# A product moved between two engines, three row passes moved by ten steps and one matmul pair issued a step earlier, in a fused selective-scan and mixture-of-experts kernel

## The chip, the cores and the metric

The kernel runs on one NeuronCore of a Trainium2 chip. The metric is the device time of one execution in microseconds (us); less is better. The engines are named as in the profile: PE (TensorE, matmuls), PEld (its weight loads), DVE (VectorE), ACT (ScalarE), POOL (GpSimd) and SP (SyncE, which issues DMAs).

## The reference

Eight sequences of 512 tokens with 256 channels. The first layer is a selective scan, the second a mixture of experts with top-1 routing and a shared expert. Cut to what matters:

```python
h = layernorm(x) * norm_w + norm_b
h = h @ in_proj_w.T                                   # 256 -> 512 channels
h = silu(causal_conv4(h, conv_w))
proj = h @ x_proj_w.T                                 # 1 + 16 + 16 columns
dt_in, B, C = proj[..., :1], proj[..., 1:17], proj[..., 17:]
dt = softplus(dt_in @ dt_proj_w.T + dt_proj_b)        # per channel
A = -exp(A_log)                                       # 512 channels x 16 states
state = exp(A * dt_t) * state + B_t * h_t             # scan over 512 tokens
y = (state * C_t).sum(states) + D * h_t
out = silu(y) @ out_proj_w.T + x
x1 = x + layernorm(out)
...
x2 = x1 + layernorm(shared(xn) + expert[argmax(xn @ gate_w)](xn * score))   # xn = layernorm(x1)
```

## The kernel before, in words

All data are fp32. The program has two stages. In the scan stage an outer loop i runs over the eight sequences (NB = 8), and in each iteration 32 steps q (Q = 32) run: two halves of the channels (2 x 128 channels each) times 16 states. The second stage, the experts, is not touched by the change.

One step q of the scan is spread over four engines. ACT makes the decays `exp(A*dt)` in PSUM (line 793, two activations, two decay buffers, made two steps ahead). The product B x h, called product q here, goes to a ring of four `bx` buffers. For the steps in `BY_POOL` (the even ones but one) POOL makes it four steps ahead, from rows of B that a DMA has broadcast (line 506). For the others DVE makes it right behind scan q - 1 (line 1114), from a row of B that PE has broadcast over the partitions into the one PSUM bank `psB` with a pair of matmuls (`spread_b`, line 1531); PE waits for DVE's product before it, since there is one bank. DVE scans (line 1126). POOL multiplies the state by C (line 517), and PE adds the states up with matmuls against an identity (`total`, line 1574), three steps behind.

Into the same 32 steps the work for the next sequence (`front`, i + 1) and for the previous one (`back`, i - 1) is written out by hand: `if q == ...` on each engine. So the order on each queue is fixed in the program, an engine does its instructions in that order, and a wait on one holds up all that stands behind it. On each engine in an iteration:

- PE: at q the loss or the spread for q + 2, then `back` at 15 and 17, then `total` for q - 3, then `front` at q. `front` 10 is the dt-in group, eight matmuls of `xp` (line 1447), `front` 18 the `w_bc` group, eight matmuls (line 1455). The `loss` for chunk c (q = 19, 21, 23, 25; lines 1522 and 1523) writes `lt - dt` into `psB` too, and the next spread waits until DVE's `min` has read it (`min_done`).
- ACT: the decays for q + 2, then at 9 the SiLUs of `front` and `back` with two table loads; at 11 and 12 two reads each of the dt-in group (`z`, line 687); at 13 to 17 softplus in five passes over 2048 elements (lines 696 to 708), the last one the `Ln` that gives `soft_ready`; at 19 first the copy of the `w_bc` group to `prow` (line 693, waits for `proj_ready`) and then the square of line 712 (`sq_ready`). For the sequence after the next (`lead`) it makes sums and squares of the rows of `xin` (line 641): sums at 3 to 6, a square at 7, three at 10.
- DVE: scan q, product q + 1 where it isn't POOL's, parts of `back` at 16, 18, 22, 24, 25, then `front`: convolution taps at 3, 5, 7 and 9 (line 1062) and the `min` of the loss at 19, 21, 23, 25 (line 1075), which waits for `loss_made` and `sq_ready`.

In i = 0 there is no `back`; in i = 7 there is no `front` and no loss, and PE does parts of the shared expert in its place (`early`, line 1552; DVE reads them at line 1104). `lead` exists in i = 0 to 5.

Of the kernel before, what the change touches and what calls it, by code (L numbers as in the profile page):

```python
# [19 lines left out]
def build(nc, x, winT, conv_w, xprojT, dt_w, dt_b, A_log, D, woutT, norm_w, norm_b,  # L20
# [16 lines left out]
    CH = C // H  # L37
    Q = H * N
    PN = N // 2
    BY_POOL = [q % 2 == 0 and q not in (14,) for q in range(Q)]  # L40
    PQ = sum(BY_POOL)
    DQ = Q - PQ
    NTH_P = [sum(BY_POOL[:q]) for q in range(Q + 1)]
    NTH_D = [q - sum(BY_POOL[:q]) for q in range(Q + 1)]
    RD = 2
# [3 lines left out]
    LOSS_AT = (19, 21, 23, 25)  # L49
# [19 lines left out]
    with ctx:  # L69
# [418 lines left out]
        def _(pool):  # L488
# [31 lines left out]
            def iteration(i, par, do_front):  # L520
                for q in range(Q):
                    if BY_POOL[(q + RB) % Q]:
                        if q + RB < Q:
# [84 lines left out]
        def _(act):  # L608
# [6 lines left out]
            def moments(i, b, mvt, scale=1.0, eps=epsc, sign=-1.0):  # L615
                nc.scalar.activation(lnv[i][:], mvt[:, :, 1], ACT.Ln, bias=eps[:], scale=scale)
                nc.scalar.activation(nmr[i][:], mvt[:, :, 0], ACT.Identity, scale=sign).then_inc(rs_ready[i], 1)
                act.wait_ge(rs_ready[i], 3 * b + 1)
                nc.scalar.activation(rstd[i][:], lnv[i][:], ACT.Exp, scale=-0.5).then_inc(rs_ready[i], 1)
                act.wait_ge(rs_ready[i], 3 * b + 2)  # L620
                for j in range(J):
                    last = nc.scalar.activation(nmr[i][:, j:j + 1], nmr[i][:, j:j + 1], ACT.Identity,
                                                scale=rstd[i][:, j:j + 1])
                last.then_inc(rs_ready[i], 1)
                act.wait_ge(rs_ready[i], 3 * b + 3)
# [3 lines left out]
            def apply(i, dst, src, js):  # L629
                for j in js:  # L630
                    last = nc.scalar.activation(dst[:, j % dst.shape[1], :], src[:, j, :], ACT.Identity,
                                                scale=rstd[i][:, j:j + 1], bias=nmr[i][:, j:j + 1])
                return last

            def lead(f, par, q):
                def row_pass(k, func, bias, dst):
                    if k == 0:
                        act.wait_ge(mv0_ready, f)
                    else:
                        act.wait_ge(row_passes, (2 * J - 1) * (f - 2) + k)  # L640
                    nc.scalar.activation(unused[:], xin[:, k % J, :], func, bias=bias,
                                         accum_out=dst).then_inc(mv0_ready if k == 2 * J - 1 else row_passes, 1)

                if q in (3, 4, 5, 6):
                    j = q - 3
                    if j == 0:
                        act.wait_ge(x_loaded, 16 * (f + 1))
                    row_pass(j, ACT.Identity, 0.0, xsum[:, j:j + 1])
                if q == 7:
                    act.wait_ge(row_passes, (2 * J - 1) * (f - 2) + J)  # L650
                    nc.scalar.activation(mv0[par][:, :, 0], xsum[:], ACT.Identity,
                                         scale=-1.0 / DIM).then_inc(mean_ready, 1)
                    act.wait_ge(mean_ready, f - 1)
                    row_pass(J, ACT.Square, mv0[par][:, 0, 0:1], mv0[par][:, 0, 1:2])
                if q == 10:
                    for j in range(1, J):
                        row_pass(J + j, ACT.Square, mv0[par][:, j, 0:1], mv0[par][:, j, 1:2])
                if q == 24:
                    act.wait_ge(mv0_ready, f + 1)
                    moments(3, f, mv0[par], (1.0 + EPS) / DIM, eps2c, 1.0)  # L660
                if q == 30:
                    if not (isinstance(f, int) and f == 0):
                        act.wait_ge(dt_ready, C * f)
                    apply(3, h1, xin, (0, 1))
                if q == 31:
                    apply(3, h1, xin, (2, 3)).then_inc(h1_ready, 1)
# [130 lines left out]
            def iteration(i, par, do_lead, do_front, do_scan, do_back):  # L797
                for q in range(Q):
# [29 lines left out]
                    if do_lead:  # L828
                        lead(i + 2, par, q)
# [190 lines left out]
        def _(dve):  # L1020
# [90 lines left out]
            def inject(i, par, q):  # L1111
                h, n = divmod(q, N)
                dve.wait_ge(b_bcast, i * DQ + NTH_D[q] + 1)
                nc.vector.tensor_tensor(bx[q % RB][:], xh[par][:, h * CH:(h + 1) * CH],  # L1114
                                        psB[:].unsqueeze(1).broadcast_to([P, CH, L]), ALU.mult).then_inc(dve_bx, 1)

            def scan(i, q):
                k = i * Q + q
                if BY_POOL[q]:
                    dve.wait_ge(pool_bx, i * PQ + NTH_P[q] + 1)  # L1120
                else:
                    dve.wait_ge(dve_bx, i * DQ + NTH_D[q] + 1)
                dve.wait_ge(decay_ready, k + 1)
                if not (isinstance(k, int) and k < RS):
                    dve.wait_ge(summed, k - RS + 1)
                nc.vector.tensor_tensor_scan(st[q % RS][:].rearrange("p c t -> p (c t)"),  # L1126
                                             decay[q % RD].rearrange("p c t -> p (c t)"),
                                             bx[q % RB][:].rearrange("p c t -> p (c t)"),
                                             0.0, ALU.mult, ALU.add).then_inc(scanned, 1)

            def iteration(i, par, do_lead, do_front, do_scan, do_back, do_choose=True):
                for q in range(Q):
                    if do_scan:
                        scan(i, q)
                        if q + 1 < Q and not BY_POOL[q + 1]:
                            inject(i, par, q + 1)
# [236 lines left out]
        def _(pe):  # L1373
# [144 lines left out]
            def loss(f, par, q):  # L1518
                c = LOSS_AT.index(q)
                pe.wait_ge(soft_ready, f + 1)  # L1520
                pe.wait_ge(dve_bx, (f - 1) * DQ + NTH_D[q + 1])
                nc.tensor.matmul(psB[:], ident[:], lt[:, c], start=True, stop=False)
                nc.tensor.matmul(psB[:], minus[:], dt[par][:, c], start=False, stop=True).then_inc(loss_made, 1)
# [54 lines left out]
            def total(i, par, q):  # L1578
                h, n = divmod(q, N)
                pe.wait_ge(weighted, i * Q + q + 1)  # L1580
                if n == 0 and not (isinstance(i, int) and i == 0 and h == 0):
                    pe.wait_ge(y_kept, H * i + h)
                if n == 0:
                    tiles(xh[par][:, h * CH:(h + 1) * CH], lambda half, c: dD[half, h * CH + c], True, False)
                tiles(st[q % RS], lambda half, c: ident[half, half], False, n == N - 1).then_inc(summed, 1)

            def iteration(i, par, do_front, do_scan, do_back):
                for q in range(Q):
                    if do_front and q - 1 in LOSS_AT:
                        pe.wait_ge(min_done, 2 + C * i + LOSS_AT.index(q - 1) + 1)  # L1590
                        spread_b(i, par, q + 1)
                    if do_front and q in LOSS_AT:
                        loss(i + 1, 1 - par, q)
                    elif not BY_POOL[(q + 2) % Q]:
                        if q + 2 < Q:
                            if do_scan:
                                spread_b(i, par, q + 2)
                        elif do_front:
                            spread_b(i + 1, 1 - par, q + 2 - Q)
                    if do_back and q in (15, 17):  # L1600
                        back(i - 1, q, do_front)
                    if do_scan and q >= SUM_LAG:
                        total(i, par, q - SUM_LAG)
                    elif do_back:
                        total(i - 1, 1 - par, q + Q - SUM_LAG)
                    if do_front:
                        front(i + 1, 1 - par, q)
                    else:
                        early(q)
                    if do_back and q not in (15, 17):  # L1610
                        back(i - 1, q, do_front)
                    if q == 20 and i >= 2:
                        choose(i - 2)

            first_front()
            iteration(0, 0, True, True, False)
            iteration(1, 1, True, True, True)
            for i in range(2, NB - 2):
                iteration(i, i % 2, True, True, True)
# [171 lines left out]
```

## Time and profile before

| | us |
|---|---|
| median of three runs | 1394.33 |
| lowest and highest | 1393.41 and 1395.83 |
| the profiled execution | 1393.79 |
| its span in the profile | 1392.0 |

The scan stage runs from about 50 to 972 us of the span, the experts follow. One iteration of the scan stage takes about 114 us. The mean granted clock of TensorE over the span is 0.968 of full speed. Views of the profile give idle time before an instruction and the instruction that ended it ("releaser"); where an instruction waits for several, the last one is named.

### The profile page before, as it was taken

To read this page: it belongs to the slowest core of one execution; us is meant where nothing else is said; L and a number is where in the kernel's file an instruction comes from. 1 tells how busy PE (TensorE), PEld (TensorE's weight loads), DVE (VectorE), ACT (ScalarE), POOL (GpSimd) and SP (SyncE) were. 2 spreads that over 40 slices of the span, in tenths; PEclk is the share of its full clock that TensorE was granted. 3 is DMA by queue.
4 is the path that set the end of the run, shared out by engine and by line. 5 is a ranking of instruction groups with operands and counts; after the bars stand their busy time and mean duration, and the time that the engine had idled before them with its cause. 6 is when DMAs were issued, how large, how long until landed. Compare 5 with 4: busy or idle time off the path is not lost.

```text
span 1392.0 us, 15477 instructions
## 1 busy us (share of the span) xinstructions
PE 1194.2 (86%) x4894; PEld 535.3 (38%) x4895; DVE 1069.5 (77%) x1409; ACT 796.5 (57%) x1386; POOL 1045.7 (75%) x558
## 2 busy tenths in 40 slices
PE   5668978887996996997798798898999999999995
PEld 2222223222332432432332243243545656656663
DVE  4588899999999999899999998799241116677675
ACT  5757679779778877877967875736431111111111
POOL 0579999999999999899999999989033723554453
PEclk9889999999999999999999999999999999999998
DMA  3921210330340141042034015001278522222220
GB/s 109 277 69 60 94 61 1 122 138 0 103 157 0 63 152 46 14 140 106 1 108 137 0 63 207 20 1 55 82 270 291 180 64 73 86 79 79 84 63 15
DMA packets 72068, 127.67 MB, mean 92 GB/s; under 512 B 8759, under 2 KB 48448, under 8 KB 67904
## 3 DMA queue, kind: packets, MB, share of 16 engines
q1 hardware_dynamic: 60432, 103.72, 22.2%
q0 software_dynamic: 7152, 16.81, 3.8%
q10 hardware_dynamic: 4416, 6.29, 1.3%
q8 instruction: 34, 0.56, 0.2%
q14 instruction: 34, 0.28, 0.1%
HBM read 97.79 MB, written 31.76 MB: 93 GB/s over the span
## 4 chain that ended last, share of the span: by engine, by line
PE 59%; DVE 21%; ACT 12%; issue 5%; DMA 1%; DVEq 0%; POOLq 0%; POOL 0%; ACTq 0%; SPq 0%
DVE state L1126 11%; PE psX L1697 10%; PE psY L1574 10%; PE psX L1632 5%; PE bank L1531 5%; DVE bx L1114 5%; PE bank L1487 4%; ACT psX L793 3%; PE psY L1645 3%; PE bank L1714 2%; PE psY L1714 2%; PE bank L1469 2%; PE bank L1470 2%; PE bank L1471 2%; DMA xin<-in_x 1%
## 5 line engine op out<-in xcount | busy, mean ns | idle before, releaser
L517 POOL TENSOR_TENSOR state<-state,cbc 128x1024 f32<-128x1024 f32 x256 | 599.2, 2367 | 10.2 <-DVE state L1126 10.2
L1126 DVE TENSOR_TENSOR_SCAN state<-psX,bx 128x1024 f32<-128x1024 f32 x256 | 580.9, 2282 | 25.9 <-ACT psX L793 22.2
L793 ACT ACTIVATE psX<-dt,aneg 128x511 f32<-128x511 f32 x512 | 331.3, 680 | 166.4 <-DVE state L1126 166.0
L506 POOL TENSOR_TENSOR bx<-xh,bbc 128x1024 f32<-128x1024 f32 x120 | 284.8, 2374 | 89.3 <-DVE state L1126 47.1
L1574 PE MATMUL psY<-state,ident 64*64 64x512 f32 x2048 | 268.0, 617 | 0.0
L1531 PE MATMUL bank<-prow,ident 128*128 128x512 f32 x272 | 151.0, 638 | 59.4 <-DVE bx L1114 57.5
L1114 DVE TENSOR_TENSOR bx<-xh,bank 128x1024 f32<-128x1024 f32 x136 | 162.9, 1198 | 15.4 <-PE bank L1531 15.3
L998 ACT ACTIVATE sg<-psX 128x512 f32<-128x512 f32 x39 | 23.3, 597 | 196.6 <-PE psX L1697 191.4
L1574 PEld LDWEIGHTS psY<-state,ident 64*64 64x64 f32 x2048 | 61.9, 133 | 166.3 <-issue 118.4
L1531 PEld LDWEIGHTS bank<-prow,ident 128*128 128x128 f32 x272 | 44.7, 192 | 149.5 <-DVE bx L1114 107.8
L581 POOL DMA_INDIRECT ysl<-shared_rows,idx x39 | 40.3, 1034 | 80.7 <-DVE idx L1292 75.7
L1201 DVE TENSOR_TENSOR actS<-sg,psX 128x512 f32<-128x512 f32 x28 | 19.0, 685 | 103.4 <-ACT sg L948 95.1
L1440 PE MATMUL bank<-lt,win 128*128 128x512 f32 x112 | 57.3, 636 | 26.3 <-DVE acc L1062 24.7
L1697 PE MATMUL psX<-wg,xsT 128*128 x156 | 77.2, 617 | 1.3 <-DVE xsT L1277 0.6
L1697 PE MATMUL psX<-wu,xsT 128*128 x156 | 73.3, 592 | 0.0
L590 POOL DMA_INDIRECT result<-yo,idx x39 | 40.1, 1029 | 36.9 <-DVE yo L1340 29.3
L1062 DVE SCALAR_TENSOR_TENSOR acc<-bank,cw,acc 128x511 f32<-128x511 f32 (+2 forms) x84 | 62.2, 741 | 6.1 <-ACT acc L676 4.1
L1447 PE MATMUL bank<-xh,xp 128*128 128x512 f32 x56 | 40.2, 883 | 27.1 <-ACT xh L682 27.1
L1283 DVE TENSOR_TENSOR actN<-sg,psX 128x512 f32<-128x512 f32 x39 | 26.8, 687 | 44.1 <-ACT sg L998 40.3
L948 ACT ACTIVATE sg<-psX 128x512 f32<-128x512 f32 x28 | 16.5, 596 | 76.8 <-PE psX L1632 76.8
L561 POOL COPY xrow<-ids 128x4 f32<-128x4 f32 x8 | 1.6, 201 | 77.8 <-issue 55.4
L1487 PE MATMUL bank<-wout,yv 128*128 128x256 f32 x256 | 58.0, 380 | 2.3 <-ACT yv L739 2.2
(212 smaller groups left out, 1798.2 us busy)
## 6 DMA issues: line engine op xcount, KB each, us to landing
cbc<-bc_rows SPq DMA_DIRECT2D x32, 1024.0 KB, 6.6
bbc<-bc_rows SPq DMA_DIRECT2D x16, 1024.0 KB, 6.4
slot_in<-ao SPq DMA_DIRECT2D x1, 5011.5 KB, 35.2
xsl<-slot_in SPq DMA_DIRECT2D x39, 128.5 KB
xin<-in_x SPq DMA_DIRECT2D x8, 512.0 KB, 4.1
xr<-in_x SPq DMA_DIRECT2D x8, 512.0 KB, 5.5
x_rows<-ao SPq DMA_DIRECT2D x8, 512.0 KB, 3.4
xn_rows<-xr SPq DMA_DIRECT2D x8, 512.0 KB, 3.2
```

Source lines behind the costliest of these rows:

```text
L506: nc.gpsimd.tensor_tensor(bx[q % RB][:], xh[par][:, h * CH:(h + 1) * CH], bbc[:, n // 2].unsqueeze(1).broadcast_to([P, CH, L]), ALU.mult). ...
L517: nc.gpsimd.tensor_tensor(w[:], w[:], cbc[:, n].unsqueeze(1).broadcast_to([P, CH, L]), ALU.mult).then_inc(weighted, 1)
L793: e = nc.scalar.activation(decay[q % RD][:, c, 1:L], dt[par][:, h * CH + c, 1:L], ACT.Exp, scale=aneg[:, h * CH + c, n:n + 1])
L1062: last = nc.vector.scalar_tensor_tensor(out=acc[:, c, m:L], in0=psF[:, 0:L - m], scalar=cw[:, c, TAPS - 1 - m:TAPS - m], in1=acc[:, c, m:L ...
L1114: nc.vector.tensor_tensor(bx[q % RB][:], xh[par][:, h * CH:(h + 1) * CH], psB[:].unsqueeze(1).broadcast_to([P, CH, L]), ALU.mult).then_inc ...
L1126: nc.vector.tensor_tensor_scan(st[q % RS][:].rearrange("p c t -> p (c t)"), decay[q % RD].rearrange("p c t -> p (c t)"), bx[q % RB][:].rea ...
L1440: last = nc.tensor.matmul(psF[:], win[:, k, c * P:(c + 1) * P], hT[:, k], start=(k == 0), stop=(k == KC - 1))
L1487: last = nc.tensor.matmul(psF[:, (j % 2) * DIM:(j % 2 + 1) * DIM], yv[:, c, j * P:(j + 1) * P], wout[:, c], start=(c == 0), stop=(c == C - 1))
L1531: nc.tensor.matmul(psB[:], ident[:, n:n + 1].broadcast_to([P, P]), prow[par][:], start=True, stop=True).then_inc(b_bcast, 1)
L1574: done = nc.tensor.matmul(psY[o * HP:(o + 1) * HP, r], weights(half, c), src[half, c], start=first, stop=last_)
L1632: last = nc.tensor.matmul(bank, w[:, k, c * P:(c + 1) * P], xg[g % 2][:, k], start=(k == 0), stop=(k == KC - 1))
L1697: last = nc.tensor.matmul(bank, xsT[i][:, k], w[:, bass.ds(ereg[i], 1), k].rearrange("p a n -> p (a n)"), start=(k == 0), stop=(k == KC - 1))
```

## The change

Three edits in the scan stage:

1. The one even step whose product DVE makes is 12 instead of 14. So POOL makes product 14, and PE spreads B for step 12 (issued at step 10) and no longer for step 14 (issued at step 12).
2. The three squares of `lead` on ACT stand at step 20 instead of step 10.
3. On PE the loss of chunk 0 (q = 19) is issued at step 18, behind `total` and ahead of `front` 18, instead of at the beginning of step 19. It keeps its waits: `soft_ready`, and DVE's products up to 19.

```diff
-    BY_POOL = [q % 2 == 0 and q not in (14,) for q in range(Q)]
+    BY_POOL = [q % 2 == 0 and q not in (12,) for q in range(Q)]
...
-                if q == 10:
+                if q == 20:
                     for j in range(1, J):
                         row_pass(J + j, ACT.Square, mv0[par][:, j, 0:1], mv0[par][:, j, 1:2])
...
                     if do_front and q in LOSS_AT:
-                        loss(i + 1, 1 - par, q)
+                        if q > LOSS_AT[0]:
+                            loss(i + 1, 1 - par, q)
                     elif not BY_POOL[(q + 2) % Q]:
...
                     elif do_back:
                         total(i - 1, 1 - par, q + Q - SUM_LAG)
+                    if do_front and q == LOSS_AT[0] - 1:
+                        loss(i + 1, 1 - par, q + 1)
                     if do_front:
                         front(i + 1, 1 - par, q)
```

## Rows read from the trace of the kernel before

**Rows 1.** The page, busy time of each engine over the span.

```profile
PE 1194.2 (86%) x4894; PEld 535.3 (38%) x4895; DVE 1069.5 (77%) x1409; ACT 796.5 (57%) x1386; POOL 1045.7 (75%) x558
```

**Rows 2.** Who waited for whom: us in total, times, longest.

```profile
DVE lt L1075 <- ACT yv L712: 20.4, 7, 3.0
```

**Rows 3.** Timeline of DVE, i = 3: start, duration, instruction, [idle before <-releaser].

```profile
439.73 1.20 DVE L1114 TENSOR_TENSOR bx<-xh,bank 128x1024 f32<-128x1024 f32 x1
...
444.47 2.29 DVE L1126 TENSOR_TENSOR_SCAN state<-psX,bx 128x1024 f32<-128x1024 f32 x1 [1.21 <-ACT psX L793]
446.68 1.20 DVE L1114 TENSOR_TENSOR bx<-xh,bank 128x1024 f32<-128x1024 f32 x1
...
473.99 0.69 DVE L1075 SCALAR_TENSOR_TENSOR lt<-bank,yv 128x512 f32<-128x512 f32 x1 [2.90 <-ACT yv L712]
```

**Rows 4.** Timeline of PE, i = 3, around the dt-in group.

```profile
434.20 1.95 PE L1574 MATMUL psY<-state,ident 64*64 64x512 f32 x16
440.02 5.31 PE L1447 MATMUL bank<-xh,xp 128*128 128x512 f32 x8 [3.88 <-ACT xh L682]
445.17 1.02 PE L1531 MATMUL bank<-prow,ident 128*128 128x512 f32 x2
```

**Rows 5.** Windows: stretch, length, busy times, granted clock, DMA share, GB/s.

```profile
440.00:441.40 1.40, 1.38 (x2) 0.84 (x3) 1.37 (x2) 1.40 (x1) 1.40 (x2) 0.50 0.00 0
```

**Rows 6.** Timeline of PE, the dt-in group in i = 0, 2 and 5.

```profile
100.20 6.25 PE L1447 MATMUL bank<-xh,xp 128*128 128x512 f32 x8 [3.87 <-ACT xh L682]
...
324.97 6.51 PE L1447 MATMUL bank<-xh,xp 128*128 128x512 f32 x8 [3.88 <-ACT xh L682]
...
669.02 5.16 PE L1447 MATMUL bank<-xh,xp 128*128 128x512 f32 x8 [3.88 <-ACT xh L682]
```

**Rows 7.** Timeline of PE, i = 3, from the `w_bc` group on.

```profile
467.57 3.70 PE L1455 MATMUL bank<-xh,w_bc 128*128 128x512 f32 x8
471.11 1.02 PE L1522 MATMUL bank<-lt,ident 128*128 128x512 f32 x2
...
472.92 1.09 PE L1574 MATMUL psY<-xh,dD 64*64 64x512 f32 x8
```

**Rows 8.** Timeline of DVE, product 13 in i = 2 and scan 12 in i = 5.

```profile
332.38 1.22 DVE L1114 TENSOR_TENSOR bx<-xh,bank 128x1024 f32<-128x1024 f32 x1 [0.67 <-PE bank L1531]
...
673.82 2.29 DVE L1126 TENSOR_TENSOR_SCAN state<-psX,bx 128x1024 f32<-128x1024 f32 x1 [1.57 <-ACT psX L793]
```

**Rows 9.** Timeline of ACT, i = 3, steps 17 to 21.

```profile
464.58 1.91 ACT L708 ACTIVATE dt<-lt 128x2048 f32<-128x2048 f32 x1
...
471.12 1.30 ACT L793 ACTIVATE psX<-dt,aneg 128x511 f32<-128x511 f32 x2 [2.33 <-DVE state L1126]
472.36 0.58 ACT L693 ACTIVATE prow<-bank 128x512 f32<-128x512 f32 x1
472.84 1.05 ACT L712 ACTIVATE yv<-tmp 128x1024 f32<-128x1024 f32 x1
...
480.41 1.30 ACT L793 ACTIVATE psX<-dt,aneg 128x511 f32<-128x511 f32 x2 [0.76 <-DVE state L1126]
```

**Rows 10.** Timeline of DVE, i = 0: product 13 and the first `min`.

```profile
107.36 1.22 DVE L1114 TENSOR_TENSOR bx<-xh,bank 128x1024 f32<-128x1024 f32 x1 [1.73 <-PE bank L1531]
...
132.03 0.69 DVE L1075 SCALAR_TENSOR_TENSOR lt<-bank,yv 128x512 f32<-128x512 f32 x1 [3.02 <-ACT yv L712]
```

**Rows 11.** Timeline of DVE, i = 7: scan 12 and the second read of `early`.

```profile
903.55 2.29 DVE L1126 TENSOR_TENSOR_SCAN state<-psX,bx 128x1024 f32<-128x1024 f32 x1 [3.44 <-ACT psX L793]
...
912.77 0.69 DVE L1104 TENSOR_TENSOR acc<-bank,acc 128x512 f32<-128x512 f32 x1 [1.90 <-PE bank L1552]
```

**Rows 12.** Timeline of ACT, i = 3: the first of three squares, then decays 13.

```profile
444.32 0.49 ACT L641 ACTIVATE unused<-xin,mv 128x256 bf16<-128x256 f32 x1
...
446.08 1.28 ACT L793 ACTIVATE psX<-dt,aneg 128x511 f32<-128x511 f32 x2
```

**Rows 13.** Timeline of ACT, i = 0: the `Ln`.

```profile
125.19 1.90 ACT L708 ACTIVATE dt<-lt 128x2048 f32<-128x2048 f32 x1
```

## The prediction

> **What bounds the kernel now.** I read the page's busy shares first [rows 1], then the list of waits [rows 2], then the timelines of DVE, PE and ACT over one steady iteration of the outer loop (i = 3, from 398 to 512 us), and last the same places in i = 0 and i = 7. PE has the largest busy time over the whole span, but the change lies in the scan stage, and there the timelines show DVE nearly without a gap: every scan and every product follows the one before within 0.1 us, save at a few places. PE, ACT and POOL have gaps in each iteration. What DVE waits for in that stage is therefore what the time is made of. In i = 3 its large gaps are 1.21 us before scan 12 and 2.90 us before the first `min` [rows 3]. No gap of DVE's names POOL.
>
> First place. Scan 12 waits for its decays, which ACT makes late because the two SiLUs and two table loads of step 9 stand ahead of them. Product 13 follows without a wait [rows 3]. On PE the eight `xp` matmuls of `front`, step 10 (the dt-in group), run from 440.02, and the spread for product 13 only after them, at 445.17 [rows 4]; that is 1.5 us before DVE wants it. In that window TensorE's granted clock is 0.50 of full speed, the 1.2 GHz level, after 3.88 us in which PE did nothing [rows 4, 5]. The group takes 5.16 to 6.51 us over the seven iterations that have it [rows 4, 6] and about 3.7 us would be its time at 2.4 GHz, as the equally large `w_bc` group shows [rows 7]. Where it took 6.51 us, product 13 also waited 0.67 us [rows 8]. The mean gap of DVE at this place over i = 1 to 6 is 1.45 us: 1.2 in three, 1.6 in two (one of them is shown), 1.21 + 0.67 in one [rows 3, 8].
>
> Second place. DVE waits for `sq_ready`, not for the loss: ACT ends decays 21, copies `prow` and then squares, up to 473.9 [rows 9, 3]. The loss of chunk 0 has ended by 472.9, when PE's next group begins [rows 7]. The wait occurs in all seven iterations with a front, 20.4 us in all [rows 2].
>
> **The change, part by part.**
>
> *Product 12 to DVE, product 14 to POOL.* DVE's work per iteration is the same, 17 products of 1.20 us; so is POOL's. What moves is a spread on PE. Spread 12 is now issued at step 10, ahead of `total` and of the dt-in group, and it waits for product 11, which ends at 440.93 [rows 3]. All that stands behind it on PE waits too: `total` 7 (about 1.0 us, half of the 1.95 us for two [rows 4]) and the dt-in group, which could otherwise start at 440.02. Spread 13 needs product 12 and stands behind the dt-in group. I work this out for i = 3. PE starts at 441.0. At full clock: spread 12 takes 1.05, `total` 7 1.0, dt-in to the next group 3.55, spread 13 to the start of the product 1.05. Sum 6.65, so 447.65. To this comes half of the time that PE runs at half clock. From the duration of the group (half clock time = 2 x (duration - 3.70)) it was 2.9 us at least (5.16), 5.6 at most (6.51), and 4.1 in the mean of the seven. So product 13 can start at 447.65 + 2.05 = 449.7 (449.1 to 450.45).
>
> On DVE scan 11 ends at 443.2, product 12 then fills the gap until decays 12 are there (444.4), scan 12 ends at 446.7 as before, and product 13 now waits until 449.7: 3.0 us (2.4 to 3.8). Against the 1.45 us of before this is +1.55 us per iteration (+1.0 to +2.35): 9.5 us over i = 1 to 6. I take the mean since the row of each end is one of seven. In i = 0 there was no gap at scan 12 and 1.73 us at product 13 [rows 10]. By the same sum product 13 starts 9.2 us after 101.2 with the 5.1 us of half clock that its 6.25 us group shows [rows 6], at 110.4; scan 12 would end at 106.9; a wait of 3.5, thus +1.8.
>
> A rule of the Trainium skill bears on this ("TensorE: Matmul & The Clock Gate", Part 1, The HAM clock gate): the array's default is the throttled state at 1.2 GHz, only activity releases it, and how many matmuls run slow differs between runs with the phase in which they begin. The trace agrees: 0.50 granted, and 5.16 to 6.51 us for one and the same group. With PE at full clock the wait would be 1.0 us and this edit would gain 0.45 us per iteration.
>
> In i = 7 the dt-in group is absent. The gap before scan 12 is 3.44 us there, and product 12 fits in: 1.2 us less later on. PE then no longer has to do spread 14 between the second and third `shu` group, for which DVE waited 1.90 us [rows 11]. That gives up to -3.1; bounds 0 and -3.1. I take -3.0, since both gaps are in the rows and spread 12, which waits for product 11 only, has all of scan 11 to run in.
>
> POOL makes product 14 as soon as scan 10 is over, about 439.8 to 442.2, well ahead of scan 14. Scan 14 no longer has a product before it on DVE; decays 14 are due about 451.6, when the dt-in group (ends about 448.8) has been read twice by ACT, ahead of scan 14 at 453. Cost 0; if this cover went, scan 14 would wait what decays 14 are late.
>
> *The squares from step 10 to step 20.* Three row passes take 1.76 us of ACT (444.32 to 446.08) [rows 12]. At step 10 they delay nothing DVE waits for: decays 13 end at 447.36, and product 13 is over at 447.88. At step 20 ACT has 0.76 us idle before decays 23 [rows 9], so decays 23, the second square and the apply of step 21 come 1.0 us later. They are hidden by scan 22, product 23 and DVE's wait-free run behind them; I take 0. If this cover failed, 1.0 us in each of the five iterations with lead and back, +5. A gain is excluded, as step 10 is followed by a wait for the dt-in group in any case. No DMA moves: the next load of `xin` waits for `h1_ready` of step 31.
>
> *The loss of chunk 0 ahead of `front` 18.* Nothing is gained by an earlier loss, as `sq_ready` ends the wait. What the four matmuls delay is the `w_bc` group: it ran 467.57 to 471.2, the loss 471.11 to 472.92, 1.81 us [rows 7]. With the order turned the `w_bc` group ends at 473.05, and the `prow` copy, which began at 472.36 behind decays 21, begins at 473.1: +0.74 us for the copy, the square and the `min`. These stand in one queue on ACT. So +0.74 us per iteration, 4.4 us over six; bounds 0 (if some of it were made up) and 1.81 (no slack at all). The loss now also waits for `soft_ready`, the end of ACT's `Ln` [rows 9], and if that is late, `w_bc` is late behind it. In i = 3 the `Ln` ends at 466.4 and PE comes to the loss at 467.6. The delays of the first edit move PE by 1.6 and ACT by about the same (1.6 to 2.1), so 0.7 us of cover remain or more. In i = 0 PE comes there earlier, and `Ln` ends at 127.1 [rows 13]. Late by some 2.3 us more (my estimate, between DVE's 1.8 and the 3.0 of the dt-in group), it lets the loss start at 129.4; with 1.85 + 3.65 + 0.48 + 1.05 for loss, `w_bc`, copy and square the `min` starts at 136.5 against 132.0 [rows 10]: 4.4 in all, 2.6 of it by this edit beyond the 1.8 above.
>
> The sum: 9.5 + 1.8 - 3.0 + 0 + 4.4 + 2.6 = 15.3 us. Later gaps of DVE, at scan 30 and product 31, come from PE groups that start with DVE's products and so move along; nothing is given back there. What follows the scan stage moves as a whole. On the profiled execution's own 1393.8 us this makes 1409 us. The median of the three runs shown is 0.5 us above that execution.
>
> **The rivals.**
>
> *Faster: product 12 fills an empty place and product 13 isn't late.* For it speaks that the 1.21 us gap is real, and that spread 13 was over (446.2) 0.5 us before its use. Against it, PE's order: spread 13 is behind 3.7 us of matmuls that begin after 443. It decides if spread 13 is done by 446.7, that is if the dt-in group ends by 445.7. Then 6 x 1.45 + 1.7 + 3.0 = 13.4 are gained, 7.0 lost by the loss: 1387 us.
>
> *The clock stays at 2.4 GHz.* PE would be idle 5.7 us before 441, longer than the 3.88 us after which it was at half; so little speaks for it. Then the first edit gives 6 x -0.45, about -0.8 and -3.0, together -6.5 against +7.0: 1394 us.
>
> *The early loss costs nothing,* because ACT finds other slack: 1409 - 7 = 1402 us. Against it, copy and square are back to back [rows 9].
>
> *The dt chain on ACT becomes the bound.* If `Ln` ends more than 0.7 us later against PE than worked out, each iteration has loss, `w_bc`, copy and square behind it. With 1.2 us more in six iterations, or with the squares of step 20 not covered: 1415 to 1419 us.
>
> **How the numbers follow.** Forecast case 0.70 (1402 to 1417), the faster rival 0.07, full clock 0.05, loss free 0.08, dt chain 0.10. Less than 0.2% (2.8 us) can't be told from no change in a measurement of this kernel. Slower: 0.70 + 0.08 + 0.10 = 0.88; the same 0.05; faster 0.07. The bounds of the terms, taken together, give +7 to +26; as they would hardly all fall on one side, the range is 1399 to 1417.
>
> **What would show it.** In the profile after, DVE should have no gap before scan 12 and one of 2.4 to 3.8 us before product 13, released by PE's spread, in i = 1 to 6. PE should be idle about 5.7 us before spread 12, with the clock at 0.5 behind it. The gap before the first `min` should be 3.6 us instead of 2.9, still released by the square of ACT, and more than 5 us in i = 0. In i = 7 the gap before scan 12 should be 2.2 us. The prediction is wrong if product 13 follows scan 12 at once, or if the `prow` copy begins with the end of decays 21.

## The result, and the profile after

The changed kernel takes 1422.94 us (median of four executions, 1417.17 to 1428.37) against 1394.76 us of the kernel before: ratio 1.0202, 95% interval 1.0146 to 1.0258. It is slower, as forecast, but by 28 us where 15 were forecast, and above the range of 1399 to 1417. The four executions lie in two groups, 1417.2 and 1417.7, 1428.2 and 1428.4. The profiled one is of the first: 1417.67 us, span 1415.9, which is 23.9 more than the span before.

What the prediction asked for is there in i = 3. Timeline of DVE in the changed kernel; the columns are start, duration, instruction and, in brackets, the idle time before it and what ended it:

```profile
403.91 2.29 DVE L1126 TENSOR_TENSOR_SCAN state<-psX,bx 128x1024 f32<-128x1024 f32 x1 [0.77 <-ACT psX L793]
...
458.85 1.22 DVE L1114 TENSOR_TENSOR bx<-xh,bank 128x1024 f32<-128x1024 f32 x1 [2.39 <-PE bank L1531]
...
485.63 0.69 DVE L1075 SCALAR_TENSOR_TENSOR lt<-bank,yv 128x512 f32<-128x512 f32 x1 [3.60 <-ACT yv L712]
...
520.29 2.29 DVE L1126 TENSOR_TENSOR_SCAN state<-psX,bx 128x1024 f32<-128x1024 f32 x1 [0.77 <-ACT psX L793]
...
576.72 1.22 DVE L1114 TENSOR_TENSOR bx<-xh,bank 128x1024 f32<-128x1024 f32 x1 [3.88 <-PE bank L1531]
...
589.94 0.69 DVE L1084 TENSOR_TENSOR ao<-bank,ao 128x512 f32<-128x512 f32 x1 [0.77 <-PE bank L1487]
...
605.13 0.69 DVE L1075 SCALAR_TENSOR_TENSOR lt<-bank,yv 128x512 f32<-128x512 f32 x1 [4.08 <-ACT yv L712]
```

The gap before scan 12 [rows 3] is gone. Product 13 waits 2.39 us for PE's spread, and the first `min` waits 3.60 us for the square instead of 2.90 [rows 3]. The first and the fourth line are scan 30 of i = 2 and of i = 3: an iteration of 116.38 us. The last three lines belong to i = 4. Product 13 waits 3.88 there, DVE's `add` behind product 17 waits 0.77 for the out-projection, which it did not before, and the `min` waits 4.08. That iteration takes 119.50 us, 3.1 more than i = 3. Of these, 1.5 are the longer wait of product 13; the waits of two `add`s (0.77 and 0.20, none in i = 3) and the longer one of the `min` are another 1.45.

PE shows what differs. Its timeline, i = 3 and then i = 4:

```profile
450.69 2.07 PE L1531 MATMUL bank<-prow,ident 128*128 128x512 f32 x2 [5.70 <-DVE bx L1114]
...
454.25 3.70 PE L1447 MATMUL bank<-xh,xp 128*128 128x512 f32 x8
...
465.75 1.12 PE L1531 MATMUL bank<-prow,ident 128*128 128x512 f32 x2 [2.12 <-DVE bx L1114]
...
567.07 2.07 PE L1531 MATMUL bank<-prow,ident 128*128 128x512 f32 x2 [5.70 <-DVE bx L1114]
...
570.98 4.84 PE L1447 MATMUL bank<-xh,xp 128*128 128x512 f32 x8
...
583.61 2.08 PE L1531 MATMUL bank<-prow,ident 128*128 128x512 f32 x2 [2.12 <-DVE bx L1114]
...
585.48 4.35 PE L1487 MATMUL bank<-wout,yv 128*128 128x256 f32 x16
```

In both, PE is idle 5.70 us ahead of spread 12, as worked out. The dt-in group then runs for 3.70 us in the one and 4.84 us in the other. And in both PE is idle 2.12 us ahead of spread 17. In i = 3 that spread takes 1.12 us, in i = 4 2.08. The windows of the changed kernel there (stretch, length, PE busy, granted clock, DMA share, GB/s):

```profile
465.70:467.00 1.30, 1.25 (x4) 1.00 0.00 0
...
583.60:584.60 1.00, 0.99 (x1) 0.50 0.00 0
```

The clock has fallen to 1.2 GHz a second time, in i = 4 to 6 but not in i = 1 to 3. The same instructions in the same order make an iteration of either kind. In what follows, a long iteration is one with this second fall.

The lengths of the iterations, from scan 30 to scan 30, and what each adds to the span (i = 0 is the shift of scan 30 in it, i = 7 the rest up to the end):

| | i=0 | 1 | 2 | 3 | 4 | 5 | 6 | i=7 | sum |
|---|---|---|---|---|---|---|---|---|---|
| before, us | | 113.68 | 114.96 | 114.27 | 114.74 | 114.62 | 114.27 | | |
| after, us | | 117.01 | 116.60 | 116.38 | 119.50 | 119.47 | 119.23 | | |
| difference | +4.7 | +3.3 | +1.6 | +2.1 | +4.8 | +4.9 | +5.0 | -2.5 | +23.9 |
| forecast | +4.4 | +2.3 | +2.3 | +2.3 | +2.3 | +2.3 | +2.3 | -3.0 | +15.3 |

For i = 0 and i = 7 the timeline of DVE after the change has:

```profile
136.76 0.69 DVE L1075 SCALAR_TENSOR_TENSOR lt<-bank,yv 128x512 f32<-128x512 f32 x1 [5.67 <-ACT yv L712]
...
930.52 2.29 DVE L1126 TENSOR_TENSOR_SCAN state<-psX,bx 128x1024 f32<-128x1024 f32 x1 [2.33 <-issue]
```

against 3.02 us [rows 10] and 3.44 us [rows 11]. The wait of 1.90 us for the second `shu` group [rows 11] is gone.

### The profile page after: what moved, and what is told of

It reads as the page before. It is cut to its first block, busy times and chain, and to the rows that moved or that the text cites. A ratio compares the mean times of both kernels' runs of the same rounds, so it can differ in the third digit from the quotient of the medians.

```text
span 1415.9 us, 15477 instructions
## 1 busy us (share of the span) xinstructions
PE 1198.8 (85%) x4894; PEld 535.7 (38%) x4895; DVE 1069.9 (76%) x1409; ACT 797.0 (56%) x1386; POOL 1045.6 (74%) x558
## 4 chain that ended last, share of the span: by engine, by line
PE 58%; DVE 23%; ACT 11%; issue 5%; DMA 2%; DVEq 0%; POOLq 0%; POOL 0%; ACTq 0%; SPq 0%
DVE state L1126 13%; PE psX L1700 10%; PE psY L1574 8%; PE bank L1531 5%; PE psX L1635 5%; DVE bx L1114 4%; PE bank L1487 4%; ACT psX L793 3%; PE psY L1648 3%; PE psY L1717 2%; PE bank L1717 2%; DVE acc L1062 2%; PE bank L1469 2%; PE bank L1447 2%; PE bank L1455 2%
## 5 line engine op out<-in xcount | busy, mean ns | idle before, releaser
L1574 PE MATMUL psY<-state,ident 64*64 64x512 f32 x2048 | 272.6, 627 | 0.0
L1531 PE MATMUL bank<-prow,ident 128*128 128x512 f32 x272 | 161.2, 677 | 102.2 <-DVE bx L1114 94.8
L1487 PEld LDWEIGHTS bank<-wout,yv 128*128 128x128 f32 x256 | 50.5, 198 | 18.6 <-issue 9.2
```

Of the source, the lines that this page charges most:

```text
L1487: last = nc.tensor.matmul(psF[:, (j % 2) * DIM:(j % 2 + 1) * DIM], yv[:, c, j * P:(j + 1) * P], wout[:, c], start=(c == 0), stop=(c == C - 1))
L1531: nc.tensor.matmul(psB[:], ident[:, n:n + 1].broadcast_to([P, P]), prow[par][:], start=True, stop=True).then_inc(b_bcast, 1)
L1574: done = nc.tensor.matmul(psY[o * HP:(o + 1) * HP, r], weights(half, c), src[half, c], start=first, stop=last_)
```

## The experiments

### One edit at a time

Each of these three kernels is the kernel before with one of the three parts of the diff.

> Only product 12 goes to DVE and product 14 to POOL. Theory: this edit alone carries the larger part of the loss, through two steps: product 13 waits 2.4 to 3.9 us behind the dt-in group, and in some iterations PE, idle 2.1 us before spread 17, falls to 1.2 GHz once more and comes late with the out-projection. +9 to +18 us against the kernel before, with a spread between executions. Rival: the second fall of the clock needs the early loss as well; then +8 us and no more, in every execution.

Measured: 1404.28 us, ratio 1.0067 (1.0054 to 1.0080), +9.2 us. Timeline of DVE, product 13 and the first `min` in i = 3:

```profile
457.23 1.22 DVE L1114 TENSOR_TENSOR bx<-xh,bank 128x1024 f32<-128x1024 f32 x1 [3.08 <-PE bank L1531]
...
483.31 0.69 DVE L1075 SCALAR_TENSOR_TENSOR lt<-bank,yv 128x512 f32<-128x512 f32 x1 [2.90 <-ACT yv L712]
```

Product 13 waits about 3 us, which was the mean forecast. The forecast for this edit was +8.3. No iteration is long: they take 115.47, 116.26, 116.20, 116.13, 116.08 and 116.06 us, although PE is idle 2.12 us ahead of each spread 17. The executions lie within 1403.6 to 1406.0. So this edit alone doesn't bring the second fall in the profiled execution, and the rival stated for this run holds, 1 us above its "no more".

> Only the three squares move from step 10 to 20. Theory: hidden at both places, within 2 us of the kernel before. Rival: the apply of step 21 comes late for DVE's add of step 22 and costs up to 1 us in each of five iterations, +3 to +5 us.

Measured: 1396.48 us, ratio 1.0011 (1.0003 to 1.0020), +1.4 us. The forecast was 0. In i = 1 DVE's `add` of step 22 waits for the apply that now stands behind the squares:

```profile
256.90 0.69 DVE L1094 TENSOR_TENSOR ao<-bank,xr 128x512 f32<-128x512 f32 x1 [0.56 <-ACT bank L631]
```

From the first `min` to scan 30 it takes 34.67 us there against 34.01 before, and 34.66 against 34.48 in i = 3: 0.66 + 4 x 0.18 = 1.4 us.

> Only the loss of chunk 0 goes ahead of the w_bc group. Theory: the prow copy on ACT begins 0.7 us later, and so the square and the min: gap of DVE before the first min 3.6 us instead of 2.9 in i = 1 to 6, some 5 us in i = 0; +6 to +7 us in all. Rival: ACT makes the delay up, and the run is within 2 us of the kernel before.

Measured: 1402.49 us, ratio 1.0055 (1.0042 to 1.0068), +7.4 us. The forecast for this edit was +7.0. The gap before the first `min` is that forecast, in each of i = 1 to 6; in i = 0 it was 8.18 us in the profiled execution, more than expected (5.2 us more than before, where 2.6 were stated for this edit). That execution is the longest of the five (1405.6), so the agreement of 7.4 with 7.0 is partly luck:

```profile
138.46 0.69 DVE L1075 SCALAR_TENSOR_TENSOR lt<-bank,yv 128x512 f32<-128x512 f32 x1 [8.18 <-ACT yv L712]
...
482.29 0.69 DVE L1075 SCALAR_TENSOR_TENSOR lt<-bank,yv 128x512 f32<-128x512 f32 x1 [3.60 <-ACT yv L712]
```

One by one the edits cost 9.2 + 1.4 + 7.4 = 18 us. Together they cost 22 to 34. What is missing is in the combination.

### Is it the clock?

```diff
+                    if do_front and q == 10:
+                        pe.wait_ge(conv_done, C * (i + 2))
+                        for _ in range(4):
+                            nc.tensor.matmul(psF[:], ident[:], win[:, 0, 0:512], start=True, stop=True)
```

> The changed kernel, and ahead of spread 12 PE does four idle matmuls of 512 columns into the free bank, whose results are overwritten, so that its clock doesn't fall there. Theory: the clock is the larger part of the product-13 wait (expected 1.0 us instead of 2.4 to 3.9) and of the second fall; 1396 to 1402 us. Rival: the order of PE's work by itself makes product 13 late, whatever the clock; 1409 us or more.

Measured: 1403.42 us, ratio 1.0063 (1.0050 to 1.0076). That is 14 to 25 us less than the changed kernel, by adding work. In i = 1 and 3 the clock holds, and product 13 waits what was worked out for the full clock, 1.0 us:

```profile
455.67 1.22 DVE L1114 TENSOR_TENSOR bx<-xh,bank 128x1024 f32<-128x1024 f32 x1 [1.02 <-PE bank L1531]
```

In i = 0, 2, 4 and 5 the gap before the idle matmuls is enough for the clock to fall; product 12 waits 0.6 to 0.7 us there, product 13 1.96. No iteration is long. The theory is right on the mechanism and a little too hopeful on the time (1396 to 1402).

> The changed kernel unchanged, for more executions and another profile. The profile so far has iterations of two lengths: about 116.5 us (i = 1 to 3) and 119.5 us (i = 4 to 6), the long ones with a second fall of the clock ahead of spread 17. Theory: executions differ in how many iterations are long: times between 1409 us (none) and 1429 us (all six), most at either end. Rival: the long executions lose their time somewhere else, for instance in the expert stage; then a profile of one shows the same iterations as before.

Measured: 1419.04 us, ratio 1.0182 (1.0155 to 1.0210). Four executions lie between 1417.9 and 1419.4, one at 1428.3, and none at 1409. The new profile is of one at 1419.4 and has the same three long iterations, i = 4 to 6 (119.63, 119.51 and 119.24 us). So in the shorter executions the pattern repeats and isn't drawn anew each time, against the first half of the theory. But three of the nine executions of this kernel take 1428 us, and none of them was profiled. The mean granted clock of each is on record: 0.958 in all three, 0.962 to 0.964 in the six shorter ones. So they spent more of their time at half clock.

```diff
+                    if do_front and q == 15:
+                        pe.wait_ge(z_done, i + 2)
+                        for _ in range(2):
+                            nc.tensor.matmul(psF[:], ident[:], win[:, 0, 0:512], start=True, stop=True)
```

> The changed kernel, and ahead of spread 17 PE does two idle matmuls of 512 columns into the free bank, so that the 2.1 us in which it waited for product 15 are filled. Theory: no second fall, all iterations about 116.5 us, 1409 to 1413 us with under 5 us between executions. Rival: the 3 us of the long iterations come from the late dt chain on ACT and not from PE's clock; then 1417 to 1428 us stay.

Measured: 1412.95 us (1411.1 to 1414.3), ratio 1.0128 (1.0112 to 1.0143). Timeline of PE in i = 4; L1592 are the two inserted matmuls, with spread 17 and the out-projection behind them:

```profile
571.36 4.86 PE L1447 MATMUL bank<-xh,xp 128*128 128x512 f32 x8
...
581.82 1.98 PE L1592 MATMUL bank<-win,ident 128*128 128x512 f32 x4
584.01 1.12 PE L1531 MATMUL bank<-prow,ident 128*128 128x512 f32 x2 [0.21 <-DVE bx L1114]
584.97 3.62 PE L1487 MATMUL bank<-wout,yv 128*128 128x256 f32 x16
```

The dt-in group is as slow as in the long iteration of the changed kernel (4.86 us, and product 13 waits 3.90 us), but spread 17 and the out-projection run at full clock. The iteration takes 117.90 us, no other takes more than 117.3. This shows what the second fall does: without it i = 4 takes 117.90 us and not 119.5, and i = 5 and 6 take 116.98 and 116.32 and not 119.5 and 119.2. The 1.5 us by which product 13 waits longer in i = 4 stay, as they stand ahead of the filled gap, but they no longer return in full in the next iterations (2.98 and 2.21 us of wait, against 3.86 and 3.50). It is 6 us against the median of the changed kernel's repetition (1419.04), and there is no second group among the four executions.

The same idea on the kernel before, with three matmuls at step 10:

> The kernel before with three idle matmuls on PE ahead of the dt-in group, so that this group runs at 2.4 GHz. Theory: the dt-in group is no bound there but in i = 0, 2 and 4 (waits of 1.7, 0.7 and 0.4 us), so 1391 to 1394 us. Rival: the idle matmuls delay total 6 or the dt-in group itself, and the time is the same or 1 to 3 us longer.

Measured: 1398.3 us, ratio 1.0018 (1.0009 to 1.0027). No gain; the rival was right: 3 us longer in the median. The profiled execution is the shortest (1395.7). Its timeline of PE in i = 2:

```profile
322.19 4.54 PE L1592 MATMUL bank<-win,ident 128*128 128x512 f32 x6 [2.39 <-DVE acc L1062]
...
327.67 3.70 PE L1447 MATMUL bank<-xh,xp 128*128 128x512 f32 x8
```

The dt-in group does run at full clock, 3.70 us where it took 6.51 [rows 6]. But the idle matmuls themselves take 4.54 us ahead of it, and product 13 waits 1.00 us behind it, 0.67 before [rows 8]. Over i = 1 to 6 product 13 waits 3.6 us in all, against 1.0 in the kernel before; only in i = 0 it waits less (0.63 against 1.73).

### Which of the edits brings the long iterations

The next kernel has parts 1 and 3 of the diff and leaves the squares at step 10.

> Product 12 to DVE and the early loss, without the move of the squares. The edits one by one gave +9.2, +1.4 and +7.4 us, together 18, and the changed kernel has +23 to +34. Theory: the second fall depends only on where in its rhythm the clock gate meets the gap ahead of spread 17, and this changes with every edit that changes the length of an iteration; so this kernel lies at 1411 to 1414 us, or has long iterations too. Rival: the squares at step 20 are needed for the long iterations because they delay ACT; then 1412 us in every execution.

Measured: 1408.1 us (1407.0 to 1409.1), ratio 1.0092 (1.0077 to 1.0108), below both numbers expected, and 3.8 us less than the 9.2 + 7.4 us of the two edits alone would give. No long iteration. The lengths are 116.85, 116.89, 116.51, 116.33, 116.19, 116.12 us: they fall from one to the next, and with them the wait of product 13, from 3.64 us in i = 1 to 2.45 in i = 5. So the move of the squares, which by itself costs 1.4 us, costs 9 to 20 us on top of the other two.

The next two add two or four statistics instructions in i = 0 to this kernel, the third adds two to the changed kernel:

```diff
+                        if isinstance(i, int) and i == 0 and q == 15:
+                            for k in range(2):
+                                nc.vector.bn_stats(out=bst[1][:, k, :], in_=xh[0][:, k, :])
```

> Product 12 on DVE and the early loss, without the move of the squares, and two statistics instructions of DVE on data that nobody reads, behind scan 15 of i = 0 only, about 1.4 us. They shift all later iterations against the rhythm of the clock gate and cost 1.4 us once. Theory: whether an iteration is long depends on this phase alone, so long iterations (119.5 us, a second fall ahead of spread 17) can appear without any change of the squares: a time above 1408 + 1.4 + 3 us, or, where this shift leads away from it, 1409 to 1410 us. Rival: the squares at step 20 are needed for them; then 1409.5 us and no long iteration in this run and in the one with four instructions.

> As the run before with four such instructions, about 2.8 us once. Theory: at least one of the two shifts brings long iterations, and then 1414 us or more. Rival: 1411 us and no long iteration.

> The changed kernel with the two statistics instructions in i = 0, 1.4 us later. Theory: with another phase the number of long iterations is another one than three (none: about 1411 us; all six: about 1429 us). Rival: the long iterations are i = 4 to 6 again, because something in these iterations itself makes them long; then 1419 us.

Measured: 1409.67 us, 1409.2 us and 1419.1 us (ratios 1.0107, 1.0104 and 1.0172). There is no long iteration in the first two, and the lengths again settle (116.11 and 116.08 us in i = 6). In the third the long ones are i = 4 to 6 again. So a shift of 1.4 or 2.8 us at the start does not decide it; my theory is wrong for these executions.

Two theories were left: the squares lengthen the iteration by 0.2 us, so that it doesn't settle at about 116.1 us; or it matters that they stand on ACT there. The next two kernels lengthen the iterations with the squares at step 10, by statistics over 64 and over 256 elements in every iteration with a front:

```diff
+                        if do_front and q == 22:
+                            nc.vector.bn_stats(out=bst[1][:, 0, :], in_=xh[par][:, 0, 0:64])
```

> Product 12 on DVE and the early loss, squares at step 10, and in each iteration with a front one statistics instruction of DVE over 64 elements on data that nobody reads, behind scan 22 (some 0.2 us, as much as the squares cost). Theory: it is the length of an iteration that brings the long ones, so they appear: 1415 us or more. Rival: only squares on ACT at step 20 bring them; then 1408 + 7 x 0.2 = 1410 us.

Measured: 1414.13 us (1414.1 to 1416.1), ratio 1.0143 (1.0127 to 1.0158). Timeline of DVE, the added instruction in i = 4, and product 13, the `add` and the `min` of i = 5:

```profile
610.75 0.20 DVE L1136 BATCH_NORM_STATS2 bst<-xh 128x6 f32<-128x64 f32 x1
610.87 1.20 DVE L1114 TENSOR_TENSOR bx<-xh,bank 128x1024 f32<-128x1024 f32 x1
...
692.38 1.22 DVE L1114 TENSOR_TENSOR bx<-xh,bank 128x1024 f32<-128x1024 f32 x1 [3.96 <-PE bank L1533]
705.64 0.69 DVE L1084 TENSOR_TENSOR ao<-bank,ao 128x512 f32<-128x512 f32 x1 [0.81 <-PE bank L1489]
...
720.83 0.69 DVE L1075 SCALAR_TENSOR_TENSOR lt<-bank,yv 128x512 f32<-128x512 f32 x1 [4.08 <-ACT yv L712]
```

An instruction that moves the next one by 0.12 us makes i = 5 and 6 long: the lengths are 116.84, 116.88, 116.56, 116.30, 119.52, 119.47 us. PE has the mark of the changed kernel:

```profile
699.27 2.08 PE L1533 MATMUL bank<-prow,ident 128*128 128x512 f32 x2 [2.12 <-DVE bx L1114]
```

Seven times 0.12 us have cost 6 us (the ratio to the kernel before is 1.0143, and 1.0092 without the instruction). (Line numbers of this kernel are up to two higher, by the added lines.)

> The same over 256 elements (about 0.35 us). Theory: long iterations from an earlier iteration on, 1418 us or more. Rival: 1411 us.

Measured: 1415.02 us, ratio 1.0147 (1.0131 to 1.0162). The long iteration comes earlier, in i = 4 (119.61 us), as the theory says. But then i = 5 takes 117.89 us and i = 6 116.97, so it isn't worse in all; the 1418 us or more did not come. How i = 4 and i = 5 differ is shown further down.

> The changed kernel with the three squares at step 23 instead of 20, behind the apply that DVE's add waits for, where ACT has room. Theory: they no longer lengthen the iteration, no long iterations, 1408 us as without their move. Rival: late squares bring long iterations wherever they stand; 1417 us or more.

Measured: 1408.22 us (1407.7 to 1411.1), ratio 1.0095 (1.0079 to 1.0110). The squares are later still and there is no long iteration (117.01, 116.97, 116.56, 116.35, 116.20, 116.13 us). Together with the run with statistics over 64 elements, this shows that the added length brings the long ones, and not the place of the squares on ACT. One digit in the changed kernel (`q == 23` for `q == 20`) takes 11 us off its median of 1419.

> Product 12 on DVE and squares at step 20, without the early loss. Theory: the length of the iterations of the first edit alone settles at 116.06 us; with 0.2 us more it may no longer, and long iterations appear: 1409 us or more. Rival: they need the early loss too; 1404.3 + 1.4 = 1405.7 us.

Measured: 1405.6 us, ratio 1.0079 (1.0065 to 1.0092), which is the sum of the two edits, and no long iteration; the rival holds. Without the early loss, 0.2 us more is still taken up: the lengths stay between 115.9 and 116.2 us, and product 13 waits less (2.42 to 3.03 us, against 2.60 to 3.22 with the first edit alone).

The traces of these runs show how the lengths come about. Behind the idle time ahead of spread 12 the clock is at half until it rises, and the longer that takes from the start of spread 12 on, the longer product 13 waits. Where narrow windows go from 0.50 to 1.00 is the time of the rise. For i = 3 and i = 4 of the changed kernel (stretch, length, PE busy, granted clock, DMA share, GB/s):

```profile
453.50:453.80 0.30, 0.30 (x8) 0.50 0.00 0
453.90:454.20 0.30, 0.30 (x4) 1.00 0.00 0
...
573.00:573.30 0.30, 0.30 (x2) 0.50 0.00 0
573.40:573.70 0.30, 0.30 (x2) 1.00 0.00 0
```

| changed kernel | i=1 | 2 | 3 | 4 | 5 | 6 |
|---|---|---|---|---|---|---|
| rise of the clock, us | 221.73 | 337.78 | 453.84 | 573.30 | 692.77 | 812.24 |
| spread 12 starts ahead of it by | 4.78 | 3.78 | 3.15 | 6.24 | 6.20 | 6.20 |
| product 13 waits | 3.16 | 2.70 | 2.39 | 3.88 | 3.86 | 3.50 |

(In i = 6 scan 12 itself waits too, 0.45 us, so product 13's wait is shorter.) In i = 1 to 3 the rises are 116.05 us apart while the iterations take 117.0 to 116.4 us. So spread 12 comes closer to the rise each time, and the wait shrinks. Then a rise comes 119.5 us after the last one, spread 12 again has a long stretch at half clock, and from there rises and iterations both go by 119.5 us. In the kernels that settle (product 12 and the early loss with or without instructions in i = 0, and the squares at step 23) the rises stay 116.05 us apart in i = 1 to 6, and the iterations come down to 116.1 us. With spread 12 about 3.1 us ahead of the rise, the kernel with the squares at step 10 takes 116.12 us, and the changed kernel still 116.38. That an iteration settles where it gets down to the distance of the rises, and otherwise slips until a rise comes later, is my reading of these rows; why a rise comes when it does no run shows.

The second fall goes by the same rise. There are twelve spreads 17 at half clock in the traces (three each in the two profiles of the changed kernel and in the one with two instructions in i = 0, two and one in the kernels with statistics over 64 and 256 elements). All twelve start 10.22 to 10.33 us after the rise. The 72 others with the same 2.12 us of idle time ahead of them start 10.37 us after it or later. The kernel with 256 elements has one of each, in i = 4 and i = 5, 10.29 and 10.37 us after the rise:

```profile
584.44 2.07 PE L1533 MATMUL bank<-prow,ident 128*128 128x512 f32 x2 [2.12 <-DVE bx L1114]
...
703.98 1.12 PE L1533 MATMUL bank<-prow,ident 128*128 128x512 f32 x2 [2.12 <-DVE bx L1114]
```

### A version that should have beaten both

```diff
-                if q == 19:
+                if q == 18:      # ACT: the square of line 712
...
-                    if do_choose and q == 21:      # DVE, and ahead of back
+                    if do_choose and q == 22:
...
-                    if q == 20 and i >= 2:         # PE
+                    if q == 21 and i >= 2:
```

> The kernel before with the square of step 19 on ACT moved to step 18, where ACT is idle 2.3 us, and the router's matmuls and their copy one step later (21 and 22), so that PE comes to the second loss sooner. Theory: the first min waits for the loss instead of the square, 0.9 us less, and the second min no longer for PE; 0.6 to 1.3 us less in each of six iterations, 1387 to 1392 us. Rival: PE is busy without a gap from spread 17 to the second loss, so the gain comes back as a wait for spread 23 or the second min: within 2 us of the kernel before.

Measured: 1401.43 us, ratio 1.0046 (1.0034 to 1.0058), +6.5 us. Timeline of DVE, i = 3:

```profile
472.07 0.69 DVE L1075 SCALAR_TENSOR_TENSOR lt<-bank,yv 128x512 f32<-128x512 f32 x1 [1.93 <-PE bank L1523]
...
482.23 1.22 DVE L1114 TENSOR_TENSOR bx<-xh,bank 128x1024 f32<-128x1024 f32 x1 [0.90 <-PE bank L1531]
...
484.74 0.69 DVE L1094 TENSOR_TENSOR ao<-bank,xr 128x512 f32<-128x512 f32 x1 [1.20 <-ACT bank L631]
```

The first gap shrinks by 0.97 us as planned, and the 0.28 us of the second `min` are gone. But PE has no gap from the second loss to spread 23 and makes product 23 wait 0.90 us, and the `add` waits 1.20 us for the apply; both waits were zero before. That is 0.85 us more in such an iteration, and neither of the two expected times came. That the apply is late because of the later router was not tried by itself. No kernel of this study beats the one before.

## Why the prediction was right and wrong

Right: the direction, the two places and their causes. Product 13 behind the dt-in group: 2.39 to 3.16 us of wait in i = 1 to 3 (2.4 to 3.8 stated; 3.88, 3.86 and 3.50 in i = 4 to 6), 5.70 us of idle PE ahead of spread 12, granted clock 0.5 behind it. The `prow` copy pushed back by the `w_bc` group, the first `min` after 3.60 us (3.6 stated) and 5.67 in i = 0 (more than 5 stated). In i = 7 a gap of 2.33 us (2.2 stated), and -2.5 us in all where -3.0 was taken. The edits alone measured +9.2 and +7.4 us for stated +8.3 and +7.0. In i = 1 to 3 they add 7.1 us together, 6.9 were stated; the squares' share was not in the 6.9, so this is closer than the terms deserve. (The term of 9.5 us should be 6 x 1.55 = 9.3.)

Wrong, first step: "I take 0" for the squares. The cover of the `add` of step 22 was 0.18 us short in i = 2 to 5 and 0.66 short in i = 1. The prediction named this price and its place but laid it on the wrong side. By itself it is a term of 1.4 us.

Wrong, second step, and the one that broke the range: the term of the first edit, +9.5 us over i = 1 to 6, counted product 13's wait alone, and all else in those iterations stood at nothing ("nothing is given back there"). The prediction followed the spread that the edit adds ahead of the dt-in group, but not what the one it takes away leaves behind. Without product 14 on DVE, PE has nothing to do between `total` 12 and product 15, a gap of 2.12 us in each iteration. I had counted the missing spread as a gain in i = 7 and as nothing elsewhere. In three iterations of the profiled execution the clock fell to 1.2 GHz in that gap, and spread 17 and the first part of the out-projection ran slow (2.08 for 1.12 us, 4.35 for 3.62). The three take 7.7 us more than forecast: 4.4 are the waits of the `add`s and the `min` behind this second fall (1.45 in each), 2.2 are product 13's wait beyond the 3.0 us taken, and about 1 is left, with the squares in it. The half clock time was treated as a random term with the mean of seven samples, but it isn't random: it goes with the length of the iteration. With product 12 on DVE and the early loss, the kernels without the 0.2 us settle at iterations of about 116.1 us with ever less half clock time; with it they pass on to iterations of 119.5 us. Shown is that filling the gap removes the second fall, that 0.12 us on another engine brings it, and that hiding the squares removes it; that the iterations settle or slip against rises of the clock 116.05 us apart is a reading of the traces.

The Trainium skill's rule ("TensorE: Matmul & The Clock Gate", Part 1, The HAM clock gate), that the number of slow matmuls depends on the phase, was cited. The traces agree within one execution too: the dt-in group takes 3.70 us in i = 3 and 4.84 in i = 4. By the runs here this dependence carries from one iteration to the next, as the rows on the rise of the clock show.

Of the rivals, the one that the `dt` chain on ACT becomes the bound gave 1415 to 1419 us and fits the time of the first group, but by luck and not by its mechanism: in i = 4 ACT waits for PE (1.10 us for the `w_bc` group ahead of the `prow` copy), not PE for ACT:

```profile
603.48 0.60 ACT L693 ACTIVATE prow<-bank 128x512 f32<-128x512 f32 x1 [1.10 <-PE bank L1455]
```

Open: what an execution of 1428 us looks like. Three more long iterations of 3.1 us would be 9.3 of its 10.7 us, and its lower mean clock (0.958) fits, but this is only worked out, as no profile caught one. So the profiled execution accounts for 8.6 of the 13.9 us between the forecast of 1409 and the median, and the rest, which comes from these executions, stays unexplained in part. Open too is why the clock rises and falls when it does, and what of the 3 us of the three idle matmuls is not product 13's wait.

## What to carry to other kernels

Moving work off an engine that is in the middle of the chain opens a gap on it. Ask of each gap, the new ones too, what state the engine is in behind it; on TensorE a gap of 2.1 us has cost 1.6 us in the iteration where the clock fell in it, and up to 3 us in those behind it. In a loop with a fixed order such a cost can repeat in every round, and 0.1 us on some other engine may decide if it does, so single edits do not add up: run the combination, and look at the lengths of the rounds one after the other rather than at the mean.

An instruction put "into idle time" ahead of a group is paid by what is queued behind it. Before giving an engine's early result (here the loss) priority, ask what really ended the wait, and whether that (here the copy and the square) is behind the work that is now pushed back.

## What was not expected of the hardware

The same 2.12 us gap on PE, with the same instructions around it, leaves the granted clock at 1.00 in one iteration and at 0.50 in the next, and in these traces the spread behind it starts at most 10.33 us after the last rise of the clock in the one case and at least 10.37 us in the other. The iteration lengths converge: 116.89, 116.51, 116.33, 116.19, 116.12 us without the move of the squares, and to 116.1 us too from two other starts (two or four instructions more in i = 0), and with it they are 119.50, 119.47, 119.23 from i = 4 on. Adding four useless matmuls to PE in each iteration with a front (eight records in the profile) made the changed kernel 14 us faster or more.
